# Router in groups of four tiles, the last pair of x loaded turned, and later loads of the first weights

## The reference

```python
w = weights[conditions]                         # (32, 64, 64)
xf = einsum('bct,bcd->bdt', x, w)               # conditioned rows, 2048 x 512
logits = xf @ Wr.T                              # 8 experts
gate = softmax(logits); top2_val, top2_idx = top_k(gate, 2)
rank = (cumsum(onehot, axis=0) * onehot).sum(-1)
keep = rank <= cap                              # cap = 640 tokens for each expert
comb[tok, flat_idx] += where(keep, flat_val, 0)
g = silu(xf @ Wg[e].T); u = xf @ Wu[e].T        # inner width 352
y = sum_e comb[:, e] * ((g * u) @ Wd[e].T)
return x + y
```

## Time and profile before

| | |
|---|---|
| median of three runs | 273.88 us (273.08 to 276.12) |
| the profiled execution | 272.44 us |
| its span, first to last instruction | 270.6 us |
| mean granted TensorE clock | 0.991 of full |
| TensorE matmul busy | 257.8 us, 95% |
| VectorE busy | 161.6 us, 60% |
| ScalarE busy | 137.7 us, 51% |
| GpSimd busy | 173.6 us, 64% |
| moved by DMA | 59.00 MB, mean 218 GB/s |
| x loads (8 of 512 KB), median to landing | 7.6 us |
| stores of conditioned rows (7 of 512 KB), median to landing | 3.0 us |

### The profile page before, as it was taken

One profiled execution on the slowest core, in us unless ns is written; L12 is line 12 of the kernel. 1 busy time (PEld: TensorE's weight loads), 2 busy tenths in 40 slices (PEclk: granted clock), 3 DMA queues, 4 the chain that ended last, 5 costly groups with the idle time before them and its releaser, 6 DMA issues.

```text
span 270.6 us, 4016 instructions
## 1 busy us (share of the span) xinstructions
PE 257.8 (95%) x1368; PEld 200.0 (74%) x1368; DVE 161.6 (60%) x332; ACT 137.7 (51%) x242; POOL 173.6 (64%) x156
## 2 busy tenths in 40 slices
PE   8999698999999999999999999999999999999991
PEld 4663156999987867888878887777787777878980
DVE  2658998444459664876566639674865867343251
ACT  2356843444464656565366644664565559442100
POOL 5792048741158867884887478858887886685742
PEclk9999979999999999999999999999999999999998
DMA  6996888999869998899679867998899699366441
GB/s 201 363 300 241 344 270 272 386 338 330 294 193 209 202 207 256 162 216 277 170 130 250 238 178 111 200 294 251 154 238 329 148 192 225 40 79 81 131 177 46
DMA packets 27099, 59.00 MB, mean 218 GB/s; under 512 B 6198, under 2 KB 6454, under 8 KB 26976
## 3 DMA queue, kind: packets, MB, share of 16 engines
q1 hardware_dynamic: 16416, 37.89, 44.3%
q0 software_dynamic: 10656, 20.75, 37.2%
HBM read 39.56 MB, written 20.25 MB: 221 GB/s over the span
## 4 chain that ended last, share of the span: by engine, by line
PE 52%; DVE 3%; ACT 2%; DMA 2%; issue 2%; POOLq 0%; ACTq 0%; DVEq 0%
PE bank L1342 19%; PE bank L1429 17%; PE bank L1437 9%; PE bank L1316 3%; DMA xg<-xf_dram,src_turn 2%; PE bank L1444 2%; PE bank L1452 2%; DVE w L1005 1%; ACT hhi L696 1%; POOLq L85 0%; DVE squares L1054 0%; PE bank L1303 0%; DVE hlo L1060 0%; DVE h L1120 0%; DVE h_last L1100 0%
## 5 line engine op out<-in xcount | busy, mean ns | idle before, releaser
L1429 PE MATMUL bank<-xhi,w 128*128 128x512 f32 x280 | 71.6, 398 | 0.0
L1342 PE MATMUL bank<-w,hhi 128*128 128x512 f32 (+1 forms) x216 | 67.1, 393 | 1.5 <-ACT y_sb L667 1.0
L554 POOL DMA_INDIRECT out<-y_sb,dst_row x35 | 56.5, 1613 | 13.4 <-issue 13.4
L1429 PEld LDWEIGHTS bank<-xhi,w 128*128 128x128 f32 x280 | 52.3, 188 | 13.2 <-DVE h_last L1100 0.8
L520 POOL DMA_INDIRECT gate_g<-gates_dram,src_row x40 | 46.8, 1170 | 12.1 <-issue 11.5
L1342 PEld LDWEIGHTS bank<-w,hhi 128*128 128x128 f32 x216 | 39.2, 188 | 10.7 <-DVE hlo L1060 1.6
L1005 DVE TENSOR_TENSOR w<-raw,w 128x704 fp32r<-128x704 f32 (+1 forms) x35 | 37.1, 1060 | 14.6 <-ACT w L609 8.2
L508 POOL DMA_INDIRECT xg<-xf_dram,src_turn x24 | 25.6, 1065 | 26.0 <-DVE xlo L990 11.6
L1342 PE MATMUL bank<-w,hlo 128*128 128x512 f32 (+1 forms) x108 | 41.9, 388 | 0.0
L1437 PE MATMUL bank<-xlo,w 128*128 128x512 f32 x140 | 38.4, 396 | 0.0
L609 ACT ACTIVATE w<-raw 128x704 fp32r<-128x704 f32 (+1 forms) x40 | 36.7, 923 | 0.0
(11 more groups left out here) (138 smaller groups left out, 304.8 us busy)
## 6 DMA issues: line engine op xcount, KB each, us to landing
raw<-wgu SPq DMA_DIRECT2D x32, 352.0 KB, 7.8
xg<-squares SPq DMA_DIRECT2D x24, 256.0 KB, 7.5
x_sb<-x SPq DMA_DIRECT2D x8, 512.0 KB, 7.6
raw<-wd SPq DMA_DIRECT2D x8, 512.0 KB
xf_dram<-xf_sb SPq DMA_DIRECT2D x7, 512.0 KB, 3.0
raw<-wd SPq DMA_DIRECT2D x8, 192.0 KB
out<-x SPq DMA_DIRECT2D x1, 1280.0 KB, 18.3
gate_g<-gates_dram,src_row POOLq DMA_INDIRECT x40, 6.5
```

The source lines that it names most:

```text
L554: nc.gpsimd.indirect_dma_start(out=out[:, :], in_=y_sb[:, n % TPE, :], in_offset=None, out_offset=bass.IndirectOffsetOnAxis(ap=dst_row[:, ...
L1342: last = nc.tensor.matmul(ps[:, cols], left(c), w[:, half, part, o:o + width], start=(c == 0 and q == 0), stop=(closes and c == cs[-1] and ...
L1429: last = nc.tensor.matmul(ACC_BANK[what][:, :], columns(what, k, part), xhi4[:, k, :], start=(k == 0 and part == 0), stop=False)
```

## The change

Five things change.

1. **Groups of four.** router, xrT_copy, turn and xr_sum work on four tiles at a time (g in place of m), and all groups of LG have four tiles.
2. **Twelve slots.** Turned tiles go to turned_x, which has RING = 12 slots for tiles 0 to 13 and two more for the last pair. It lies where memory of the experts is not used yet. pick_p stays in turned_sb.
3. **The last pair comes turned.** The host lays a second copy of the last two tiles of x out already turned (xt). SyncE loads it in the place of the last pair of x, and the plain last pair behind the placed conditioning matrices, together with the padding rows of xf_dram and gates_dram.
4. **Order.** TensorE turns eight tiles ahead of the first router step; condition(4) and (6) go behind the rank matmuls; condition(0) and (2) stay ahead of them. The softmax is taken in one part: its exp stands behind the fourteenth row copy, and gates() behind more.
5. **Weights.** Only units 0 and 1 of expert 0 are loaded early; units 2, 3 and 4 are issued behind the store of gates. ScalarE's w_high of units 2 and 3 stands directly ahead of x_high(0). The wait of the first gate and up matmuls is for two units, and one for all four stands ahead of units 2 and 3. KEEP_WARM goes from 18 to 26.

```diff
-BEFORE_RANKS = 4
-W0_EARLY = 1
-LG = ((0, 3), (3, 5), (5, 7), (7, NM))
+W0_EARLY = 2
+LG = ((0, 2), (2, 4), (4, 6), (6, NM))
+NG = len(LG)
+RING = 3 * XR
+TURNED = TT - 2
-KEEP_WARM = 18
+KEEP_WARM = 26
...
+        def turned_slot(j):
+            return j % RING if j < TURNED else RING + j - TURNED
...
-            for m in range(2, NM):
+            for m in range(2, NM - 1):
                 load_x(m)
-            sp.dma_start(xf_dram[N:N + 1, :], x[0:1, :]).then_inc(xf_out, 16)
-            sp.dma_start(gates_dram[N:N + 1, :], x[0:1, 0:E]).then_inc(gates_out, 16)
+            sp.dma_start(turned_x[:, RING:RING + 2, :, :],
+                         xt.rearrange("p (r k c) -> p r k c", r=2, k=KH)).then_inc(xt_in, 16)
...
             for j in range(HALF, TT):
                 place(j)
+            load_x(NM - 1)
+            sp.dma_start(xf_dram[N:N + 1, :], x[0:1, :]).then_inc(xf_out, 16)
+            sp.dma_start(gates_dram[N:N + 1, :], x[0:1, 0:E]).then_inc(gates_out, 16)
...
-            for u in range(KH):
+            for u in range(W0_EARLY):
                 load_unit(0, u)
...
-            sp.wait_ge(gates_ok, 2)
+            sp.wait_ge(gates_ok, 1)
             sp.dma_start(gates_dram[0:N, :].rearrange("(p j) e -> p j e", j=TT),
                          gate[:, :, :]).then_inc(gates_out, 16)
-            load_unit(0, KH)
+            for u in range(W0_EARLY, NU):
+                load_unit(0, u)
...
             for j in TURN_ACT:
                 act.wait_ge(tT_ps, j + 1)
-                if j >= XR:
-                    act.wait_ge(xrT_ps, j // 2 - 1)
+                if j >= RING:
+                    act.wait_ge(xrT_ps, 1)
...
-            for n in range(2):
-                xf_copy(n, n)
-            exps(0)
...
+            for n in range(TT):
+                xf_copy(n, n % XR)
+                if n == TT - 3:
+                    act.wait_ge(sub_ok, 2)
+                    nc.scalar.activation(ex[:, :, :], lg[:, :, :], ACT.Exp).then_inc(ex_ok, 1)
             for u in range(W0_EARLY):
                 w_high(u, 0, 0)
...
             nc.scalar.activation(g_sb[:, 0:1], ident[:, 0:1], ACT.Silu).then_inc(silu_warm, 1)
+            for u in range(W0_EARLY, KH):
+                w_high(u, 0, 0)
             x_high(0)
...
+            for j in TURN_DVE[0:4]:
+                turn_copy(j)
+            xrT_copy(0)
+            for j in TURN_DVE[4:]:
+                turn_copy(j)
+            xrT_copy(1)
+            xr_sum(0)
+            xrT_copy(2)
+            xr_sum(1)
+            top_two(0)
+            xrT_copy(3)
+            xr_sum(2)
+            top_two(1)
+            xr_sum(3)
...
             dve.wait_ge(consts, RANKS)
             one_hot(0)
             top_two(2)
             top_two(3)
-            subtract(GATED, LG[3][0] * 2)
             subtract(LG[3][0] * 2, TT)
             one_hot(1)
-            gates(1)
+            subtract(0, LG[3][0] * 2)
...
+            gates()
+            w0_low(0)
             dve.wait_ge(slot_ps, 1)
...
-            for u in range(W0_EARLY, KH):
+            for u in range(1, KH):
                 w0_low(u)
...
+            turn_tiles(0, 8)
+            pe.wait_ge(wr_in, 16)
+            router(0)
+            turn_tiles(8, 12)
+            router(1)
+            turn(0)
+            turn_tiles(12, TURNED)
+            router(2)
+            turn(1)
+            logits(0)
+            router(3)
+            turn(2)
+            logits(1)
             condition(0)
-            router(NM - 1)
-            turn(NM - 2)
-            condition(2)
-            turn(NM - 1)
+            turn(3)
             logits(2)
             logits(3)
-            after = EARLY_PAIRS * 2 + BEFORE_RANKS
-            for j in range(EARLY_PAIRS * 2, after, 2):
-                condition(j)
+            condition(2)
...
-            for j in range(after, TT, 2):
+            for j in range(4, TT, 2):
                 condition(j)
...
                 if s == 0:
-                    pe.wait_ge(wlo0_ok, KH)
+                    pe.wait_ge(wlo0_ok, 2)
...
+                if s == 0:
+                    pe.wait_ge(wlo0_ok, KH)
                 first_gate_up(s, n, (2, 3))
```

More of the change, by code:

```diff
@@ L1180, in x_tile_turn, with router @@
                 last.then_inc(tT_ps, 1)
-            def router(m):
-                for j in (m * 2, m * 2 + 1):
+            def router(g):
+                for j in range(g * XR, min((g + 1) * XR, TURNED)):
                     turned(j)
-                if m >= 1:
-                    pe.wait_ge(xrT_ok, m)
-                r = m * 2 % XR
+                if g == NG - 1:
+                    pe.wait_ge(xt_in, 16)
+                if g >= 1:
+                    pe.wait_ge(xrT_ok, g)
                 for k in range(KH):
-                    last = nc.tensor.matmul(ps_xrT[k * Q:(k + 1) * Q, 0:2 * P]
-                                            .rearrange("q (j c) -> q j c", j=2), wr_sb[:, k, :],
-                                            turned_sb[:, r:r + 2, k, :], start=True, stop=True)
-                last.then_inc(xrT_ps, 1)
@@ L1195, in turn @@
-            def turn(m):
-                pe.wait_ge(xrT_ok, m + 1)
-                if m >= 1:
-                    pe.wait_ge(xr_ok, m)
-                for j in range(2):
+                    if g < NG - 1:
+                        last = nc.tensor.matmul(ps_xrT[k * Q:(k + 1) * Q, :]
+                                                .rearrange("q (j c) -> q j c", j=XR),
+                                                wr_sb[:, k, :],
+                                                turned_x[:, g * XR:(g + 1) * XR, k, :],
+                                                start=True, stop=True)
+                    else:
+                        for half, r in enumerate((turned_slot(g * XR), RING)):
+                            cols = slice(half * 2 * P, (half + 1) * 2 * P)
+                            last = nc.tensor.matmul(ps_xrT[k * Q:(k + 1) * Q, cols]
+                                                    .rearrange("q (j c) -> q j c", j=2),
+                                                    wr_sb[:, k, :], turned_x[:, r:r + 2, k, :],
+                                                    start=True, stop=True)
```

111 lines of the change are left out of this document (38 added, 73 removed).

## The result

The changed kernel takes 279.76 us (median of four runs, 278.33 to 281.37) beside 273.48 us of the kernel before in the same session: a ratio of 1.0253, interval 1.0167 to 1.0339. The medians are 6.3 us apart, where 2.5 were forecast, and 279.76 lies above the range. The profiled execution took 281.37 us (span 279.6), 9.0 us of span more than the one of before; it is also the longest of the four, whose other spans are 276.6, 278.0 and 278.1. The other 1.6 lie behind it, and that much means little: from the first down matmul to the end it takes between 217.5 us (e3) and 220.7 us (e9) in the fourteen profiles of this document, 218.1 before and 219.7 after.

The account below looks back on a forecast made before the run. The first expert's start, set by the row chain, was taken to bound the kernel. Row copies 1.9 + stores 0.2 + x_low wait 0.4 = 2.5 us later than the 273.88 median: 276.4 us, range 273.8 to 278.9.

Parts of the forecast that it names:

- the row chain: Conditioning matmuls, ScalarE copies and stores of rows into xf_dram; claimed to end last and release the first gather, at 39.65.
- the list: Ranks, slots and picks up to src_row, which the gather also needs; forecast at 37.2, hidden by the rows by 2 us.
- a shift there goes to the end one for one: At the first expert's start: almost no idle time follows, so any delay there reaches the end in full.
- the signs that were named: Ranks 26.5 to 27.5, last copy 35.0 to 36.0, first gather 39 to 40.5, first turn 43.5 to 45, wait for x_low(0).
- The router: Router steps up to the rank matmul: start at 27.05 against 27.34, gain 0.3 us, between 1.5 gained and 0.8 lost.
- The order of the conditioning: Two pairs move behind the ranks, six there in place of four, paced by ScalarE: last row copy 1.9 us later.
- 28.55 + 6.8: Pair 4's copy at 28.55, then twelve copies, three bank handovers and one exp: last row copy at 35.35 against 33.46.
- I add 0.2 (0 to 0.8): Row stores between last copy and first gather: added delay in us from the backlog of six pairs in a row.
- Taken for nothing is the contention of gathers and weights: First gather beside late weight loads: counted as no delay, though the skill's rule gave up to 0.9 us.
- The wait for x_low: TensorE in the first expert waits for x_low(0), delayed by late weights: 0.8 us (0 to 2.0), half taken, 0.4.
- The first rival: Clock falls on the first expert because keep-warm ends ahead of the gathered rows: 1.7 us more, 278.1; chance 0.27.
- Both hide behind the gather: Twenty-six keep-warm matmuls end at 42.3 at full clock or 44.0 at slow; gathered rows come at 44.2, so no cost.

Follow-up runs that it names:

- e3: Changed kernel with condition(4) and (6) ahead of the rank matmuls again and all four gate and up units loaded early: 274.88 us, ratio 1.0065 to before.
- e9: e3 with 36 small matmuls of 8 columns added behind the warm-up at the start: 274.65 us, ratio 1.0043 to before.
- e2: Changed kernel with all four gate and up units of expert 0 loaded early again: 278.6 us, ratio 1.0210 to before.
- e5: Changed kernel with 16 extra matmuls of 256 columns between condition(2) and the rank matmuls: 279.75 us, ratio 1.0222 to before.
- e8: Kernel before with condition(4) and (6) behind the rank matmuls and the second exp ahead of the copies of tiles 4 and 5: 278.08 us, ratio 1.0169.
- e10: Kernel before with 36 small matmuls added behind the warm-up: ratio 1.0068 to before.
- e7: Kernel before with only the weights part of the change, units 2, 3 and down weights issued behind the row and gates stores: 277.57 us, ratio 1.0125.
- e1: Changed kernel with condition(4) and (6) ahead of the rank matmuls again: 276.26 us, ratio 1.0103 to before.
- e4: Changed kernel with 42 keep-warm matmuls in place of 26: 278.01 us, ratio 1.0144 to before.
- e12: e11 with gates() behind dst_row on VectorE in place of ahead of src_row: 274.19 us, ratio 1.0030 to before.
- e11: e9 with 18 keep-warm matmuls in place of 26: 273.71 us, ratio 1.0042 to before.

## Why the prediction was wrong

**The frame held in the main.** The start of the first expert sets the end, the row chain ends last and the list has slack: the gather of the changed kernel is released by xf_dram, the list is 3.4 us early, and of 9.0 us of span 7.4 arise up to the first down matmul. But "a shift there goes to the end one for one" failed at the place that it named: the first turned rows come 4.7 us later (46.75 against 42.09), and 2.8 more arise behind them in the first expert, which the forecast left as fast as before but for 0.4. Of the signs that were named the last copy (36.06) lies at its upper bound, the ranks (26.14), the gather (41.24) and the first turn (46.75) lie outside theirs, and the wait for x_low(0) didn't come.

**The router: right in kind, undersized.** 0.3 us of gain was forecast, in bounds up to 1.5; 1.2 came. Router 3 ended by 20.2 and not 21.1, and from there to the rank matmul it took 5.94 us, where VectorE's order had been laid out as 5.95. The 0.9 us above the forecast came through to the row chain, since all six pairs stand behind the rank matmul now; they are the only term that made the sum smaller. The order that let them through cost 3.8 us from ranks to last copy (9.92 against 6.12).

**The order of the conditioning: the step held at full clock, and its price was short.** "28.55 + 6.8" gave 8.3 us from the ranks on; e2 and e5 have 8.59. With the fall of the clock it is 9.92, in the changed kernel and in e8. The text named the 1.5 us in which TensorE idles ahead of the ranks and didn't ask what it does to the clock. This is the first term that failed, by 1.3 us, and in part by chance, since in e2 the clock stayed up behind the same stretch.

**"I add 0.2 (0 to 0.8)" for the stores failed.** 1.1 us in the changed kernel, above my upper end, and 1.4 to 2.0 in most others. A backlog is there, but little more than before (the pair stores land in 2.6 to 4.1 us, before in 2.6 to 3.9). The last store lags by one engine, as read in e3, and e9 and e10, one profile each, speak for the instruction transfer as its cause, without proving it. Where a chain fills all 16 DMA engines, a transfer of 16 KB may then cost it 1 us or more; the rows of before did not show it, since there the transfer happened to come when the stores were nearly done.

**"Taken for nothing is the contention of gathers and weights" failed.** 1.0 us from gather to turned rows in the changed kernel, 1.8 in e7 alone. The quoted rule of the Trainium skill ("DMA: Bandwidth & Descriptors", "Issuing engines are not separate DMA queues") gave an estimate of up to 0.9, the better of the two numbers: the changed kernel's trace agrees with it, and e7's 1.8 us are twice as much. The price isn't a constant: with the same late weights the stretch takes 5.45 us in e1, but 4.61 in e4 and 4.11 in e5, where the gather starts 0.9 us later than in the changed kernel, and in e12, with early weights, it takes 5.40. The DMA share of 0.70 from which I took nothing is a mean over a stretch of before in which it falls to 0.14 for a microsecond (39 to 40); the late weights fill just the part in which the gather ran nearly alone (0.88 and more from 38 to 43 in e7). **The wait for x_low**, 0.4 us, didn't come: ready at 49.19, wanted at 51.10, and in e7 47.03 and 47.95. The late gather used up the delay, and the half clock the rest.

**The first rival came, with the forecast's mechanism and not instead of it.** It had a chance of 0.27 and a price of 1.7 us; it cost 2.7 (e4: 10.43 against 13.17), because the clock stayed low for 6.8 us. The forecast had treated keep-warm as hidden ("Both hide behind the gather") and so took the gap behind it as free. But each term that makes the gather late widens that gap. The forecast itself had 1.9 us of it at full clock; the rows came 2.6 us later than its 44.2 and keep-warm ended 0.8 later than its 42.3, so it was 3.7 us. The clock fell behind all six gaps of 2.8 us and more that these profiles have there. It belonged in the sum. The Trainium skill's page "TensorE: Matmul & The Clock Gate" ("Why this matters for your kernels") had warned of such gaps, and the trace agrees.

Together, 59.92 less 55.0 is 4.9 us: 1.3 for the first fall of the clock and 0.3 for six pairs at full clock above 8.3, 0.9 for the stores, 1.0 for the gather, 2.4 for the first expert (2.8 less the 0.4 of x_low), less 0.9 for the earlier ranks (each rounded).

**By parts.** Each alone in the kernel before, the order costs 1.7% (e8) and the late weights 1.25% (e7); the rest of the change, with 26 keep-warm matmuls, 0.65% (e3), of which 0.4% stay with the transfer moved (e9) and with eight keep-warm matmuls less (e11); the intervals overlap, so the difference isn't shown. e7's 1.25% hold the fall of the clock as well: e1 and e3, which differ in the late weights alone and keep their clock up on the first expert, are 0.4 points apart (1.0103 and 1.0065, with intervals that overlap). The sum, 3.6%, is more than 2.5%, since two of them pay for the same fall of the clock on the first expert.

**Left open.** Why e11 stays 0.4% above before although its profile starts the experts earlier; whether the 16 KB transfers are TensorE's code, and how far ahead it is fetched; why the gather is held up for longer than the packet takes; and what makes the clock fall behind one idle stretch of 1.6 us (after) and not behind another (e2).

## What to carry to other kernels

Where a wait is made longer ahead of dense TensorE work, put the fall of the clock into the sum and not among the rivals: what is late and what the clock then costs are one case. Look at the slack of a chain by resource: moving two of eight equal steps behind a barrier costs their time on the pacing engine, and where the transfers keep all DMA engines busy, look also for what else is in the queues. Set a gain upstream against what the order that lets it through costs: here 1.2 us of the router reached the row chain, and the order cost it 3.8.

## What the runs showed of the hardware

A 16 KB instruction transfer holds one of the 16 DMA engines for 0.9 to 1.7 us, and where all engines are full the last of a row of stores lands 1 to 2 us later in the profiles that have it there (5.3 us in e3 against 3.3 before), which is a link and no proof of a cause. Its place moved with the instructions ahead of it: 36 matmuls of 8 columns moved it out of the stores in e9, and by 0.4 us into them in e10. The granted clock fell to half in the first expert behind idle stretches of 2.8 us and more in six of six profiles, and not behind 2.6 us (e1), 1.5 (e12) or less; behind 1.6 us ahead of the ranks it fell in after and e4 and not in e2, and behind 2.25 us there it fell in e8. In the changed kernel the low rows cover 3.6 us in one case (clock 0.53) and 6.8 in the other (0.51).
